# Shift rows of a softmax: turned by VectorE in 32x32 blocks in place of TensorE and a ring bank

## The reference

```python
q = rope((x @ wq).reshape(B, S, 16, 16)); k = rope((x @ wk).reshape(B, S, 4, 16)); v = (x @ wv).reshape(B, S, 4, 16)
scores = einsum('bqkgd,bskd->bkgqs', q.reshape(B, S, 4, 4, 16), k) / sqrt(16)
attn = softmax(scores, axis=-1)
x = layernorm(x + einsum('bkgqs,bskd->bqkgd', attn, v).reshape(B, S, 256) @ wo)
h = silu(x @ Wg.T) * (x @ Wu.T)          # Wg, Wu, Wd: integers - 128, times a scale per row
x = layernorm(x + h @ Wd.T)
```

## Time and profile before

| | |
|---|---|
| median of 3 runs | 936.12 us (935.14 to 936.33) |
| span of the profiled execution | 932.5 us |
| TensorE busy (PE) | 914.6 us, 98% |
| VectorE busy (DVE) | 753.7 us, 81% |
| ScalarE busy (ACT) | 715.2 us, 77% |
| GpSimd busy (POOL) | 249.5 us, 27% |
| DMA | 68.78 MB, mean 74 GB/s |

### The profile page before, as it was taken

One profiled execution on the slowest core, in us unless ns is written; L12 is line 12 of the kernel. 1 busy time (PEld: TensorE's weight loads), 2 busy tenths in 40 slices (PEclk: granted clock), 3 DMA queues, 4 the chain that ended last, 5 costly groups with the idle time before them and its releaser, 6 DMA issues.

```text
span 932.5 us, 15773 instructions
## 1 busy us (share of the span) xinstructions
PE 914.6 (98%) x5574; PEld 465.6 (50%) x5574; DVE 753.7 (81%) x1519; ACT 715.2 (77%) x932; POOL 249.5 (27%) x214
## 2 busy tenths in 40 slices
PE   9998999999999999999999999999999999999996
PEld 3323434343443434434344344434335888888885
DVE  5777999999999999999999999999973456655555
ACT  2456898989889988889988989898896555555564
POOL 7752565010010001001000100400101666656455
PEclk9997999999999999999999999999999999999998
DMA  7986433222133132223313133221110201101001
GB/s 258 281 227 189 96 90 84 72 69 52 43 75 80 43 66 59 51 65 70 72 42 75 46 63 70 69 51 43 32 52 15 70 24 46 46 23 46 24 24 47
DMA packets 50080, 68.78 MB, mean 74 GB/s; under 512 B 13520, under 2 KB 23760, under 8 KB 50000
## 3 DMA queue, kind: packets, MB, share of 16 engines
q1 hardware_dynamic: 49136, 64.61, 26.9%
q0 software_dynamic: 864, 3.15, 1.1%
HBM read 46.74 MB, written 16.25 MB: 68 GB/s over the span
## 4 chain that ended last, share of the span: by engine, by line
PE 92%; DVE 3%; ACT 2%; issue 1%; DMA 1%; SPq 1%; POOL 0%; POOLq 0%; DVEq 0%; ACTq 0%
PE pv_bank L1266 27%; PE ring_bank L1173 26%; PE pair_bank L1324 13%; PE pair_bank L1387 11%; PE pv_bank L1413 3%; PE ring_bank L1413 3%; PE ring_bank L1276 2%; PE pair_bank L1214 2%; ACT probs L1087 1%; PE ring_bank L1186 1%; PE ring_bank L1291 1%; PE pv_bank L1155 1%; PE ring_bank L1229 0%; DMA q_parts<-low 0%; DVE by_sin L727 0%
## 5 line engine op out<-in xcount | busy, mean ns | idle before, releaser
L1087 ACT ACTIVATE probs<-pair_bank 128x1024 f32<-128x1024 f32 x512 | 496.4, 1026 | 68.8 <-PE pair_bank L1324 67.6
L762 DVE TENSOR_REDUCE block_max<-ring_bank 128x1 f32<-128x512 f32 x732 | 468.8, 682 | 31.6 <-PE ring_bank L1173 23.7
L1173 PE MATMUL ring_bank<-k_max,q_sb 48*128 48x512 f32 x1003 | 314.8, 475 | 3.6 <-ACT above L1032 1.4
L1266 PE MATMUL pv_bank<-probs,v_all 128*32 128x512 f32 x2048 | 273.5, 606 | 0.6 <-ACT probs L1087 0.5
L1173 PEld LDWEIGHTS ring_bank<-k_max,q_sb 48*128 48x128 f32 x1003 | 136.5, 184 | 251.9 <-DVE block_max L762 127.4
L1324 PE MATMUL pair_bank<-q_sb,k_sb 50*128 50x512 f32 x1024 | 204.9, 416 | 0.9 <-ACT probs L1087 0.7
L619 POOL TENSOR_TENSOR attn<-attn,inv_rows 128x1024 f32<-128x1024 f32 x7 | 16.7, 2384 | 491.4 <-DMA inv_rows<-inv_d 491.4
L1324 PEld LDWEIGHTS pair_bank<-q_sb,k_sb 50*128 50x128 f32 x1024 | 101.2, 186 | 33.6 <-ACT probs L1087 15.1
L944 DVE SCALAR_TENSOR_TENSOR hid<-pair_bank,up_s,silu 128x512 f32<-128x512 f32 x63 | 47.1, 747 | 84.7 <-ACT silu L1134 84.7
L667 POOL TENSOR_TENSOR hid_l<-hid,hid_h 128x512 fp32r<-128x512 f32 x63 | 81.8, 1298 | 86.0 <-ACT hid_h L1113 85.3
L759 DVE CUSTOM_DVE_ANT_0 above<-ring_bank,above 128x512 f32<-128x512 f32 x137 | 94.4, 691 | 12.5 <-ACT above L1032 5.2
(11 more groups left out here) (140 smaller groups left out, 860.6 us busy)
## 6 DMA issues: line engine op xcount, KB each, us to landing
k_max<-k_parts SPq DMA_DIRECT2D x96, 96.0 KB, 3.5
q_sb<-q_parts SPq DMA_DIRECT2D x64, 128.0 KB, 3.4
k_sb<-k_parts SPq DMA_DIRECT2D x96, 64.0 KB, 2.3
attn<-xT SPq DMA_DIRECT2D x8, 512.0 KB, 5.1
q_parts<-high SPq DMA_DIRECT2D x16, 256.0 KB, 3.8
q_parts<-low SPq DMA_DIRECT2D x16, 256.0 KB, 4.1
q_sb<-q_parts SPq DMA_DIRECT2D x64, 64.0 KB, 3.5
attn<-pv_sb SPq DMA_DIRECT2D x128, 32.0 KB
```

The lines of the kernel that those rows point to most:

```text
L762: dve.reduce_max(block_max[half % 2][:, col:col + 1], bank, axis=AX.X).then_inc(ring_used, 1)
L1087: act.activation(probs[t % 2][:, 2 * pr:2 * pr + 2, :], pair_bank[pr][:], ACT.Exp, scale=D ** -0.5).then_inc(probs_ready, 1)
L1173: pe.matmul(bank, q_sb[k][rows, i, qt * P:(qt + 1) * P], k_max[k // QH][rows, kind * CH:(kind + 1) * CH], start=True, stop=True).then_inc( ...
L1266: ins = pe.matmul(pv_bank[32 * j:32 * j + 2 * D, :], v_all[:, head, t, :], probs[t % 2][:, 2 * (j % 2) + j // 2, :], start=(t == 0), stop= ...
```

## The change

The high and the low part are made in SBUF from `row_max` while it is still 128 queries x 16 columns, side by side as 128 x 32 (`shift_rows`). VectorE's transposition turns each block of 32 x 32 in place: `shift` is then 128 partitions x 32, in which partition 32 b + 16 o + c holds part o (high or low) of column c for the queries 32 b to 32 b + 31. TensorE's transposition and the ring's entry are gone. VectorE copies the high part ahead of the second block of step 5, as before, and makes the low part and the transposition after the fourth. For half 0 the three stand behind the blocks 2, 3 and 6 of half 1. `load_shift` issues 8 DMAs, for high and low x 4 blocks; each moves 16 partitions x 32 values to two partitions of `q_sb[k]`, in runs of 128 B. With one entry fewer to a half, the ring's banks turn from half to half.

```diff
-SHIFTS = 16 * GROUPS * SHIFT
+SQ = 32
+SHIFTS = 16 * SHIFT * P // SQ
-        shift = [sb(f"shift{c}", [G * QT, SHIFT, P], f32r, two) for c in range(2)]
+        shift_rows = [sb(f"shift_rows{c}", [P, SHIFT, G * QT], f32r, two) for c in range(2)]
+        shift = [sb(f"shift{c}", [P, SQ], fp32, two) for c in range(2)]
...
-            def load_shift(pair, k, split):
-                sp.wait_ge(*split)
-                for r in range(GROUPS):
-                    heads = G // GROUPS * QT
-                    for o in range(SHIFT):
-                        row = r * GROUP + ROWS + o
-                        dst = q_sb[k][row:row + 1].rearrange("o j (q p) -> o (j q) p", p=P)
-                        sp.dma_start(dst.bitcast(fp32), shift[k % 2][r * heads:(r + 1) * heads, o, :].bitcast(fp32)).then_inc(shift_loaded[k], 16)
+            def load_shift(pair, k):
+                sp.wait_ge(shift_ready, HALVES * pair + k + 1)
+                for o in range(SHIFT):
+                    for b in range(P // SQ):
+                        dst = q_sb[k][ROWS + o::GROUP].rearrange("r j (q b p) -> r (j q) b p", q=QT, p=SQ)[:, :, b, :]
+                        src = shift[k % 2][b * SQ + o * G * QT:b * SQ + (o + 1) * G * QT]
+                        sp.dma_start(dst.bitcast(fp32), src).then_inc(shift_loaded[k], 16)
...
-            def split_shift(bank, half, index, guard):
-                if guard is not None:
-                    dve.wait_ge(*guard)
-                dve.tensor_copy(shift[half % 2][:, 0, :], bank[0:G * QT, 0:P]).then_inc(shift_h_ready, 1)
-                dve.wait_ge(shift_h_ready, index + 1)
-                dve.tensor_tensor(shift[half % 2][:, 1, :], bank[0:G * QT, 0:P], shift[half % 2][:, 0, :].bitcast(fp32), ALU.subtract).then_inc(ring_used, 1)
+            def shift_high(half):
+                dve.wait_ge(row_max_ready, half + 1)
+                dve.tensor_copy(shift_rows[half % 2][:, 0, :], row_max[half % 2][:]).then_inc(shift_h_ready, 1)
+
+            def shift_low(half):
+                dve.wait_ge(shift_h_ready, half + 1)
+                dve.tensor_tensor(shift_rows[half % 2][:, 1, :], row_max[half % 2][:], shift_rows[half % 2][:, 0, :].bitcast(fp32), ALU.subtract).then_inc(shift_l_ready, 1)
+
+            def turn_shift(half):
+                dve.wait_ge(shift_l_ready, half + 1)
+                if half > 1:
+                    dve.wait_ge(shift_loaded[(half - 2) % HALVES], SHIFTS * ((half - 2) // HALVES + 1))
+                dve.transpose(shift[half % 2][:], shift_rows[half % 2][:].rearrange("p o n -> p (o n)").bitcast(fp32)).then_inc(shift_ready, 1)
...
             def maxima(g):
+                turned = shift_at(g)
                 for e in range(4):
-                    if e == 1 and split_at(g) is not None:
-                        half = split_at(g)
-                        guard = None if half < 2 else (shift_loaded[(half - 2) % HALVES], SHIFTS * ((half - 2) // HALVES + 1))
-                        split_shift(entry((half, "split")), half, half, guard)
+                    if e == 1 and turned is not None:
+                        shift_high(turned)
                     if maxima_at(g):
                         half, t = maxima_at(g)
                         take_max(half, 4 * t + e)
+                if turned is not None:
+                    shift_low(turned)
+                    turn_shift(turned)
...
-            def transpose_max(half):
-                pe.wait_ge(row_max_ready, half + 1)
-                bank = free_bank((half, "split"))
-                pe.transpose(bank[0:G * QT, 0:P], row_max[half % 2][:], ident[:]).then_inc(ring_ready, 1)
```

More of the change, by code:

```diff
@@ L29 @@
 SHIFT = 2
-SHIFTS = 16 * GROUPS * SHIFT
+SQ = 32
+SHIFTS = 16 * SHIFT * P // SQ
 QT = CH // P
 MAXES = G * QT * QH
-RING = MAXES + 1
 BANKS = 3
 LEAD = 12
-SPLIT_AT = 5
+HIGH_AT = 5
+OUT_AT = 6
 FIRST = 5
@@ L185, in layer @@
         ring_ready, ring_used, row_max_ready = sem("ring_ready"), sem("ring_used"), sem("row_max_ready")
-        shift_h_ready = sem("shift_h_ready")
+        shift_h_ready, shift_l_ready, shift_ready = sem("shift_h_ready"), sem("shift_l_ready"), sem("shift_ready")
         pv_copied = sem("pv_copied")
@@ L237, in layer @@
             where = early[(n, h) if n < BLOCKS else (BLOCKS, HOOKS - 1)]
-            if i == 2 * KT + 1:
-                where.append((0, "split"))
             where.extend(step(i))
@@ L246, in layer @@
                 for key in early[n, h]:
-                    place(key, key[0] if key[0] in ("v", "gap") else "max" if key[1] == "split" else ("above" if blocks(key[0], key[1] // 4)[key[1] % 4][1] == 2 else "max"))
+                    place(key, key[0] if key[0] in ("v", "gap") else ("above" if blocks(key[0], key[1] // 4)[key[1] % 4][1] == 2 else "max"))
         early_entries = len(readers)
@@ L253, in maxima_at, with shift_at @@
             return (half, t) if half < HALVES * PAIRS else None
-        def split_at(g):
+        def shift_at(g):
             n, t = divmod(g, KT)
-            return n + 1 if t == SPLIT_AT and n + 1 < HALVES * PAIRS else None
+            return n + 1 if t == HIGH_AT and n + 1 < HALVES * PAIRS else None
         for g in range(HALVES * PAIRS * KT):
             for e in range(4):
-                if e == 1 and split_at(g) is not None:
-                    place((split_at(g), "split"), "max")
                 if maxima_at(g):
@@ L409, in projections @@
                     if last and c == 1:
-                        load_shift(0, 0, taken_through((0, "split")))
+                        load_shift(0, 0)
                     store_q(m, 1)
@@ L489, in attention @@
                     if k < HALVES - 1:
-                        load_shift(p, k + 1, taken_through((n + 1, "split")))
+                        load_shift(p, k + 1)
                     elif not last:
-                        load_shift(p + 1, 0, taken_through((n + 1, "split")))
+                        load_shift(p + 1, 0)
                     if k % QH == 0 and not last:
@@ L791, in early_maxima @@
                     half, e = key
-                    if e == "split":
-                        split_shift(entry(key), 0, 0, None)
-                        continue
                     take_max(half, e)
@@ L797, in early_maxima @@
                         row_maxima(half)
+                    if half and e == 2:
+                        shift_high(0)
+                    if half and e == 3:
+                        shift_low(0)
+                    if half and e == 6:
+                        turn_shift(0)
             for m in range(BLOCKS):
@@ L1039, in early_takes @@
                         gap_high(key[1])
-                    elif key[1] != "split" and key[1] % 4 < 2:
+                    elif key[1] % 4 < 2:
                         difference(key[0], key[1] // 4, (key[1] % 4,))
@@ L1201, in early_work @@
                         make_gap(key[1])
-                    elif key[1] == "split":
-                        transpose_max(key[0])
                     else:
@@ L1338, in attention @@
                         if t not in MIXED:
-                            if split_at(g) is not None:
-                                transpose_max(split_at(g))
                             maxima(1)
@@ L1365, in attention @@
                                 pe.wait_ge(attn_in_ready, 4)
-                            if k == QH and t == SPLIT_AT + 1:
-                                pe.wait_ge(*taken_through((HALVES * PAIRS - 1, "split")))
-                            part = g - (KT * (HALVES * PAIRS - 2) + SPLIT_AT + 1)
+                            if k == QH and t == OUT_AT:
+                                pe.wait_ge(*taken_through((HALVES * PAIRS - 1, MAXES - 1)))
+                            part = g - (KT * (HALVES * PAIRS - 2) + OUT_AT)
                             if 0 <= part < 6:
```

## The result

The changed kernel takes 998.15 us (median of 4 runs, 991.2 to 999.97), beside 935.63 us (933.85 to 936.33) for the kernel before: the ratio is 1.064 (95% interval 1.061 to 1.067). The forecast was 1022 us, in a range of 953 to 1075.

What follows compares the result with a forecast made beforehand. The prediction took TensorE and VectorE in lockstep, both close to full, as the bound, with SP's shift-row deadline second. 936.12 us plus 64 for stalls and 23 for clock falls summed to 1023, stated as 1022; range 953 to 1075 us.

Steps and rivals of the forecast that it cites:

- The deadline: Head of step 0: TensorE stops until the shift rows land, at 21.91 us, but would ask at 19.52; 2.4 us standstill.
- a margin of 2.7 us: Before step 0 in the kernel before: shift rows there at 317.4, asked for at 320.10.
- The stall's size: Head of step 0: halves of 21.91 instead of 19.79 us, 2.12 us more in each of halves 1 to 30, 64 us.
- the term of SP's queue: SP's queue: 8 DMAs instead of 4, starts 0.69 us apart, last start 4.84 us after the first, 2.8 us later than before.
- The 1.6 us from the last issue to TensorE: End of the shift DMAs: assumed time from the last issue's start until TensorE goes on, between 1.3 and 1.8 us.
- 0.16, 0.16 and 0.21 us as estimated: VectorE's added copy, subtraction and transposition in SBUF: 0.16, 0.16 and 0.20 us plus 0.05 us of waits, 0.57 in all.
- The clock: TensorE: a standstill may lower its clock; falls of 3.5 us, 1.5 us each, in half of 30 stalls, 23 us.
- the two gaps that I went by: TensorE idle ahead of the attention: 1.2 us from 50.00 with a clock fall after it, 0.86 us from 38.00 without.
- a start put at 0 +- 2 us: Half 0: shift rows up to 1 us late against as much gained from the missing split; net 0, 2 us either side.
- The forecast's own range: Whole kernel: 985 to 1065 us, for starts 0.6 to 0.75 us apart and clock falls in none or all stalls.
- the second rival: SP's queue: starts 0.47 us apart, a stall of 0.8 us too short for the clock, 17 us more, 953 us; chance 0.07.
- The gain: TensorE and the ring: removing the transposition and ring entry saves at most 0.27 us in 31 halves, 8.4 us in all.

Runs made afterwards that it cites:

- The turn ahead of the second block: The changed kernel with the low part and the transposition moved from behind the fourth block of step 5 to ahead of the second: 938.53 us, ratio 1.000.

## Why the prediction was right, and what its sizes missed

**The deadline.** Right, and shown. TensorE waits at the head of step 0 for the DMAs in 29 of the halves 0 to 30. An earlier turn alone takes the loss away, fewer DMAs alone take the stall away, and eight DMAs alone in the kernel before cost nothing in steady halves. The mechanism was a later turn and a longer issue against a margin of 2.7 us, less the 0.27 us by which TensorE asks earlier. Measured, SP begins 1.8 us later in the half (15.26 against 13.44) and its last issue stands 1.8 us further behind its first (3.87 against 2.08): 3.6 against 2.4, and 1.2 us of standstill.

**The stall's size.** Too large: 20.70 us a half and not 21.91. Of the 1.21 us, 7 x (0.69 - 0.55) = 0.98 is the term of SP's queue, where I took the time of the old shift DMA (634 ns); the new one takes 495. The next 0.21 us is the turn, at 15.26 and not 15.47 us. The 1.6 us from the last issue to TensorE measured 1.57. In place of 64 us the stalls cost 30 x 0.91 = 27 us.

The Trainium skill's page "DMA: Bandwidth & Descriptors", section "Issuing engines are not separate DMA queues", says that the time to start a DMA is usually small beside the DMA itself. This case is not like that: one start takes 0.495 us and eight take 4.36, where TensorE goes on 1.57 us after the start of the last.

**VectorE.** 0.16, 0.16 and 0.21 us as estimated, 0.53 against 0.57. What I missed is that the copy and the subtraction now have both sides in SBUF and stand still while GpSimd works there. Before, with PSUM as the source, they took 0.27 and 0.28 us beside the same work (VectorE above, GpSimd below, in the trace of before):

```profile
154.79 0.27 DVE L771 CAST shift<-ring_bank 16x128 fp32r<-16x128 f32 x1
155.09 0.28 DVE L773 TENSOR_TENSOR shift<-ring_bank,shift 16x128 fp32r<-16x128 f32 x1
```
```profile
154.09 2.39 POOL L601 TENSOR_TENSOR down_l<-w_f,down_h 128x1024 fp32r<-128x1024 f32 x1
```

Both sides in SBUF is not the whole condition, since the reduction to `row_max` has that too and was never longer than 0.19 us. In the changed kernel the holds cost 1.4 us in halves 18, 22, 26 and 30 and more in the first eight; with GpSimd moved behind the turn the changed kernel takes 11.4 us less by the medians of two groups of runs (986.72 against 998.15), and 8.6 us by their ratios (1.055 against 1.064).

**The clock.** That a stall brings it down was right. One of the two gaps that I went by was read too short: TensorE's timeline has it idle for 1.07 us ahead of 39.20, and not for 0.86. So the gap without a fall (1.07 us), the gap with one (1.19 us) and the measured stall (1.2 us) are nearly the same length. I assumed 15 falls of 3.5 us; behind half 1 the changed kernel's trace has nine, of 3 to 17 us, and that of the kernel with GpSimd moved behind the turn has nine regular ones from half 7 on, which cost 2.7 us each and not 1.5, as they last 7 to 8 us. Two of the nine in the changed kernel (at 152 and 565 us) stand behind a held VectorE instruction and not behind a wait for the shift rows. By the 2.7 us for each 7 us or so, the 51 us that the nine last cost some 20 us (an estimate), near the 23 of the forecast, which is luck: they are fewer, and longer. With the stall filled the falls are gone, and the time is 15.6 us less (986.72 to 971.11).

**The sum.** For the profiled execution it can be read from the starts of SP's shift DMAs. From half 0 to half 30 the kernel before takes 670.14 - 73.49 = 596.65 us and the changed one 736.40 - 79.42 = 656.98, which is 60.3 more: 27.3 are the stalls (30 x 0.91), 5.7 the holds in halves 18, 22, 26 and 30, and 27.3 the falls of the clock with the holds of the first eight halves, which I can't separate in this trace; 18.8 of these lie in halves 1 to 7. Half 0 is issued 5.9 us later, the step to half 31 is 2.5 us shorter, and 1.4 us are left behind it, which makes up the 65.2 us between the spans. The forecast had 64 + 23 for these: 37 us too much for the stall, against holds that it did not know and a start put at 0 +- 2 us. That 998 is no further from 1022 is in part luck, as these have opposite signs.

Of the 5.93 us of half 0, 3.75 stand already at its row maxima (made at 72.93 against 69.18), ahead of all that the change touches; the other traces of changed kernels have them at 67.8 to 74.6. From there to SP's start it is 6.49 us, against 4.31 before: 2.18 us are the change's, some 0.6 of them a held copy (0.73 us). The first halves vary likewise: the step from half 0 to half 1 is 27.3 us in this trace, and 25.0 and 23.1 us in those of the changed kernel with the one or the other set of waits for GpSimd.

**The ranges.** The forecast's own range of 985 to 1065 us doesn't follow from the bounds named for it. Starts 0.6 us apart and no fall give 936 + 30 x 1.48 = 980 us; starts 0.75 us apart and a fall in each half give 936 + 30 x 2.53 + 45 = 1057 us. The measured starts, 0.55 us apart, lie between these bounds and the second rival's 0.47.

**The gain.** The 0.27 us a half that the ring's entry costs are real: halves fall from 19.79 to 19.51 or 19.54 us in three kernels without a stall. The 8 us that this promised came out only with GpSimd moved, 927.88 us.

## What to carry to other kernels

A rewrite of a small side path should be judged by when its result is ready against when it is needed, counting every issue on the DMA queue; here 0.3 us saved on the busy engine were paid with 4 us on a path that had 2.7 us to spare. Moving the source of VectorE's copy or subtraction from PSUM to SBUF brings it beside GpSimd's SBUF work, and the wait it then makes is shown only as a longer instruction; place GpSimd's work by a wait directly in front of it, not in front of its load. And a standstill of TensorE costs more than its length, so a filled one was worth 15 us here while it stayed a standstill.

## What the runs showed of the hardware

- VectorE's copy (128 x 16, 0.16 us) and subtraction in SBUF last until a GpSimd subtraction, product or cast on SBUF that was running before them ends: up to 2.32 us, the ends within 0.04 us of each other. A copy from PSUM of before took 269 to 279 ns in all 32 halves, and the reduction of 128 x 32 in SBUF at most 0.19 us.
- Under GpSimd's `TENSOR_SCALAR` (128 x 1024, from integers, 2.8 us) they do not wait for its end. In three traces the held one ends 1.07 us after the start of that instruction; here the copy at 99.07, with the subtraction and the transposition behind it (VectorE above, GpSimd below, in the trace of "The turn ahead of the second block"):

```profile
98.56 0.51 DVE L768 CAST shift_rows<-row_max 128x16 fp32r<-128x16 f32 x1
99.11 0.18 DVE L772 TENSOR_TENSOR shift_rows<-row_max,shift_rows 128x16 fp32r<-128x16 f32 x1
99.32 0.21 DVE L778 STREAM_TRANSPOSE shift<-shift_rows 128x32 f32<-128x32 f32 x1
```
```profile
98.00 2.79 POOL L595 TENSOR_SCALAR w_f<-w_raw 128x1024 f32<-128x1024 int32 x1 [4.86 <-DMA w_raw<-gate_w]
```

- VectorE's transposition of 128 x 32 takes 0.21 us (201 to 214 ns), and the same under a running GpSimd instruction: under the one just shown, and in the changed kernel's trace under a product (VectorE above, GpSimd below).

```profile
307.93 0.21 DVE L778 STREAM_TRANSPOSE shift<-shift_rows 128x32 f32<-128x32 f32 x1
```
```profile
307.77 2.39 POOL L617 TENSOR_TENSOR attn<-attn,inv_rows 128x1024 f32<-128x1024 f32 x1 [86.23 <-DMA inv_rows<-inv_d]
```

- The issue of a DMA from SBUF to SBUF on SP's queue is 634 ns for 8 partitions x 512 B to one partition, 573 ns for 4 partitions x 512 B, and 495 ns for 16 partitions x 128 B to two. The last two move the same 2 KB, and the one with more runs is the shorter; which property orders them was not tried.
- Behind stalls of 1.2 us the clock fell in every third half, once in the second, of the changed kernel with GpSimd moved behind the turn, with the same stall in all halves, each time for 7 to 8 us. In the changed kernel itself it did not fall from 406 to 565 us, with seven such stalls. With TensorE filled and no instruction held it did not fall once behind 93 us.
